# Moving the window block between the two halves of a gathered group, on TensorE and on VectorE

## The reference, cut to what matters

```python
def rgcn_conv(x, src, dst, etype, W, root, bias):
    seg = dst * R + etype
    agg = segment_sum(x[src], seg, n * R)
    cnt = segment_sum(ones, seg, n * R)
    agg = where(cnt > 0, agg / max(cnt, 1), 0).reshape(n, R, -1)
    return einsum('nrd,rdk->nk', agg, W) + x @ root + bias
h = relu(rgcn_conv(h, ..., W1)); h = relu(rgcn_conv(h, ..., W2)); h = relu(rgcn_conv(h, ..., W3))
```

## Time and profile before

| | us |
|---|---|
| median of 3 runs | 5267.58 |
| lowest and highest run | 5249.11, 5267.61 |
| the profiled execution | 5260.04 |
| its span, first to last instruction | 5258.3 |
| mean granted TensorE clock, as a share of full | 0.823 |

### The profile page before, as it was taken

One profiled execution on the slowest core, in us unless ns is written; L12 is line 12 of the kernel. 1 busy time (PEld: TensorE's weight loads), 2 busy tenths in 40 slices (PEclk: granted clock), 3 DMA queues, 4 the chain that ended last, 5 costly groups with the idle time before them and its releaser, 6 DMA issues.

```text
span 5258.3 us, 105311 instructions
## 1 busy us (share of the span) xinstructions
PE 3666.9 (70%) x20468; PEld 2929.5 (56%) x20688; DVE 2687.7 (51%) x6973; ACT 1162.6 (22%) x3868; POOL 2380.1 (45%) x2346
## 2 busy tenths in 40 slices
PE   4777566666777777766767677677777777584872
PEld 1233455555666666555555555566566666574862
DVE  7654344444444444355555555455554554794336
ACT  0122111111111122122222222223322322351112
POOL 0000233344455555466666666566666665002530
PEclk8999777787888888877777778788888888797986
DMA  2022222222333444322323233344444444255740
GB/s 75 33 63 68 73 61 67 74 73 81 97 101 115 121 120 123 108 76 78 86 80 84 81 90 89 105 115 117 126 124 123 129 125 115 104 208 150 203 133 13
DMA packets 478385, 526.90 MB, mean 100 GB/s; under 512 B 96596, under 2 KB 398238, under 8 KB 474670
## 3 DMA queue, kind: packets, MB, share of 16 engines
q1 hardware_dynamic: 252780, 246.52, 15.1%
q0 software_dynamic: 85824, 199.51, 14.0%
q10 hardware_dynamic: 139746, 80.46, 5.2%
HBM read 399.82 MB, written 126.39 MB: 100 GB/s over the span
## 4 chain that ended last, share of the span: by engine, by line
PE 36%; issue 20%; POOL 14%; DMA 13%; DVE 9%; DVEq 3%; ACT 2%; ACTq 1%; SPq 1%; POOLq 0%; another core or an unknown queue 0%
POOL msg_r L608 14%; DMA msg_r<-y_tab,idx_r 9%; PE psum L1566 9%; PE psum L1636 4%; PE psum L1568 2%; DMA msg_r<-x_tab,idx_r 2%; DVE shot_r L1136 2%; PE psum L1747 2%; PE psum L1709 1%; PE psum L1432 1%; PE psum L1494 1%; DVE h_t L1365 1%; PE psum L1748 1%; PE psum L1524 1%; PE psum L1506 1%
## 5 line engine op out<-in xcount | busy, mean ns | idle before, releaser
L608 POOL DMA_INDIRECT msg_r<-y_tab,idx_r x2160 | 2221.9, 1029 | 2223.9 <-issue 1161.6
L1566 PE MATMUL psum<-shot_r 128*128 128x200 f32 x2604 | 1000.1, 486 | 465.1 <-DVE shot_r L1136 437.3
L1130 DVE SCALAR_TENSOR_TENSOR shot_r<-edge_f,win_base,iota 128x600 bf16<-128x600 f32 x434 | 366.4, 844 | 1197.1 <-PE psum L1568 740.7
L684 ACT COPY idx_r<-row_i 128x1 int32 x2142 | 395.6, 190 | 2246.6 <-DMA msg_r<-y_tab,idx_r 2044.3
L1566 PEld LDWEIGHTS psum<-shot_r 128*128 128x128 f32 x2604 | 554.8, 262 | 476.5 <-issue 472.1
L1115 DVE TENSOR_SCALAR hot_r<-iota,edge_g 128x128 f32<-128x128 f32 x1602 | 454.4, 357 | 186.4 <-PE psum L1748 148.8
L1568 PEld LDWEIGHTS psum<-shot_r 128*100 128x100 bf16 x2604 | 444.7, 171 | 115.0
L1568 PE MATMUL psum<-shot_r 128*100 128x128 bf16 x2604 | 462.3, 271 | 0.0
L1747 PE MATMUL psum<-msg_r,shot_r 128*128 128x128 f32 x1440 | 338.1, 321 | 175.3 <-DMA msg_r<-y_tab,idx_r 94.6
L1636 PEld LDWEIGHTS psum<-hot_r,msg_r 128*128 128x128 f32 x2880 | 408.9, 218 | 16.7 <-DMA msg_r<-y_tab,idx_r 6.8
L1636 PE MATMUL psum<-hot_r,msg_r 128*128 128x128 f32 x2880 | 405.8, 300 | 11.3 <-DMA msg_r<-y_tab,idx_r 4.5
(11 more groups left out here) (322 smaller groups left out, 4932.6 us busy)
## 6 DMA issues: line engine op xcount, KB each, us to landing
msg_r<-in_attr SPq DMA_DIRECT2D x882, 64.0 KB
h_t<-count_tab SPq DMA_DIRECT2D x25, 1600.0 KB, 6.6
w_tab<-shot_r ACTq DMA_DIRECT2D x385, 100.0 KB
count_tab<-shot_r ACTq DMA_DIRECT2D x385, 100.0 KB
h_t<-w_tab SPq DMA_DIRECT2D x24, 1600.0 KB, 8.0
msg_r<-y_tab,idx_r POOLq DMA_INDIRECT x2160, 2.6
xn<-heavy_tab SPq DMA_DIRECT2D x76, 320.0 KB
y_tab<-y_s SPq DMA_DIRECT2D x25, 640.0 KB, 2.9
```

Of the source, the lines that this page charges most:

```text
L608: pool.indirect_dma_start(out=msg_r[:, q, 0:width], out_offset=None, in_=table, in_offset=bass.IndirectOffsetOnAxis(ap=idx_r[:, q:q + 1], ...
L684: nc.scalar.copy(idx_r[:, q:q + 1], of[:, q:q + COLS - U + 1][:, bass.ds(c0, 1)]).then_inc(s_idx[k], 1)
L1130: V.scalar_tensor_tensor(out=key_b, in0=of(KEY, KW), scalar=win_base[:, bass.ds(w, 1)], in1=to(KW), op0=ALU.subtract, op1=ALU.is_equal).th ...
L1566: T.matmul(win_ps, low_f[:, i, :], weighted_f[:, i, :], start=False, stop=False)
```

## The change

On TensorE, `window_sums` moves from before the first chunk of a group to before the fourth. On DVE, `window_hots` moves from before the first half of the scaled one-hots to before the second. Both moves are in all three passes. ACT, POOL and SP have the same instructions in the same order as before, and nothing is added or removed. The extra block of each tile in pass 1 and the left-over blocks stay where they are.

```diff
                     dve.wait_ge(s_einv_acc, p)
-                    window_hots(in_pass(dve, 0, p, D, None))
                     for h, half in halves():
+                        if h == 1:
+                            window_hots(in_pass(dve, 0, p, D, None))
                         dve.wait_ge(s_free[0], p * U + half.stop)
                         dve.wait_ge(s_inv_e[h], p)
...
                         group_columns(k, D, p, chunk, plane=slice(INV, INV + 1))
-                        window_hots(in_pass(dve, k, p, D, n_rest))
                         for h, half in halves():
+                            if h == 1:
+                                window_hots(in_pass(dve, k, p, D, n_rest))
                             dve.wait_ge(s_free[k], p * U + half.stop)
                             scaled_hots(k, half, INV).then_inc(s_hot[k][h], 1)
...
                 if k == 0:
                     inverse_counts(p, slot)
-                if k < 3:
-                    window_sums(x)
                 for q in range(U):
+                    if k < 3 and q == UH:
+                        window_sums(x)
                     if q % UH == 0:
```

## The result

The changed kernel takes 5484.0 us (median of 4 runs, 5457.7 to 5493.1) against 5258.3 us (4 runs, 5244.2 to 5267.6): a ratio of 1.0423, with a 95% interval from 1.0377 to 1.047. The profiled execution took 5481.0 us (span 5479.3), 221 more than the 5260.0 of the one before. The forecast was 5320, with a range to 5420: slower was right, the size was not.

A forecast was written before the change was run, and what follows sets the result against it. Pass 0 was taken as bound by a TensorE-DVE ring, passes 1 and 2 by POOL and what it waits for. Terms 160 - 55 - 45 = +60 us on 5260.0 gave 5320 us, range 5225 to 5420.

The forecast's parts named there:

- Pass 0, +160: Pass 0: first groups of tiles +78 us, second groups +86, inner groups -4; +135 to +226 by preparation time.
- the preparation: DVE in pass 0: register work before the block's one-hots, taken as 2.4 us behind three scaled one-hots (2.19 to 2.95).
- The inner ring: Pass 0, 72 inner groups: closed TensorE-DVE chain of 10.29 us, to change by -0.05 us and stay near 10.2.
- Pass 1, -55: Pass 1: POOL's wait before first gathers goes, smaller waits come before fourth gathers; -55 us, bounds -130 and 0.
- 24 x 5.0 going to 24 x 3.8 us: Pass 1 tile ends: wait at the extra block falls from 5.0 to 3.8 us, one block fewer before the third chunk.
- 0.7 us at half clock: Pass 1, fourth gather: loses nothing at full clock, 0.7 us at half; 96 x 0.7 x 0.44 = 30 us.
- Pass 2, -45: Pass 2: the move gains 45 us although the first chunk now waits for ACT's plain one-hots; bounds -110 and +30.
- Of the 163 us over 948 I take 45 away: Pass 2: step that takes 45 us off the 163 us by which the pass exceeds 948 us.
- the ring of two groups: Pass 2: chain from sixth landing through L705, chunks, block and gathers; fits two 7.9 us groups at full clock.
- Rival 2: Wait only moves: fourth gather waits as the first did, pass 0 pays in full; 5395 to 5486, near 5420; chance 0.15.
- Rival 1: Pass 0 inner groups: shorter gap before the block keeps TensorE's clock full, -100 us at most, 5220 us; chance 0.15.
- Rival 3: Waits of passes 1 and 2 nearly vanish (-160) against pass 0's +160, giving 5260 us; chance 0.25.

The follow-up runs named there:

- the first series: First of four measuring series, holding the first four kernels (pass 0, 1 or 2 moved alone; pass 0 with first groups old); kernel before takes 5683.5 us there.
- the late copy: Pass 2 moved, ACT copies the block out after the next group's first plain ones: 5321.0 us, 1.0122; with early attribute transfers too 5235.2 us, 0.9967.
- the early loads: Kernel before with DVE's block register loads ahead of pass 0's wait: 5161.8 us, 0.982; the same with the block moved in pass 0: 5155.6 us, 0.981.

## Why the prediction was right in one pass and wrong in another

**Pass 0, +160: right in sum and cause, partly by luck in the terms.** 166 us were measured, and 115 in the first series. The reason holds: the block's one-hots wait for L1552 and then for the preparation, and with the preparation elsewhere 15 us are left. The inner ring came out as said, 10.24 us; all inner groups together gave 13 us and not 4. Within a tile's start the sizes were off, but not their sum: forecast 17.6 and 13 us, together 30.6; found 15.8 and 15.0, together 30.8. That two errors of 2 us a tile cancel is luck; in the first series the two groups grew by 3.9 and 0.5 us (means). The delay itself was right in both groups, 5.39 and 5.40 us from L1554 to the block against 5.66 and 5.46 forecast, and so was the preparation, 2.35 us for 2.4.

**Pass 1, -55: right in kind, too large.** It gained 22 us by the two traces. Over all profiles but those of the first series the mean is 1112.2 us in four with the block moved and 1130.5 in nine with the old order, 18 us. The tile ends came out as forecast: 24 x 5.0 going to 24 x 3.8 us was the term, 137 going to 101 us was found, although ACT's index copies are now what POOL waits for there. The first gather's wait went too. What was too small is the wait put in its place: 0.7 us at half clock, 30 us in the sum, where 78 us stand before the fourth gathers, in 54 of 120 groups.

**Pass 2, -45: the step that failed.** It was "Of the 163 us over 948 I take 45 away". Measured was +81: 126 us of the 161 by which the profiled execution missed the sum (+221 against +60). The step weighed ACT's 3.3 us to L705 against the ring of two groups, within which the runs show it to be nearly free: 294 us of such waits stood in a pass of 1122.9 us. It did not look at the first and second group of a tile, where the whole loss is, nor at SP at all. There the requests for a tile's second group stand behind the waits for the tile's own loads, and the block had been the work that ran meanwhile. With the first half ahead of the block, the first chunk needs them before they are there. The second group grew by 2.7 us, 24 times 66 us, and when they were asked for early it shrank by 3.8 (12.1 to 8.2); the sum had no such term. The smaller part is ACT's order in a tile's first group, 1.3 us or 31 in all, of which the late copy gave back 21 to 32 us.

**The rivals.** Rival 2 had the size nearly (5395 to 5486, measured 5484) and the wrong place: the loss of pass 2 was not the fourth gather's wait in the middle of a tile but a transfer at its start. In pass 1 its mechanism is there inside the tiles, where 60 us before the first gathers became 78 before the fourth; what the pass gained it gained at the tile ends. Rival 1, the clock, did not come: 0.81 in pass 0 as before. But it came with the early loads. The pause ahead of the block, 2.44 us in the earlier trace rows and 1.96 after the change, fell to 0.46 us, and the clock of the pass was 0.88 and 0.90 with the block moved, 0.85 without. The Trainium skill (TensorE: Matmul & The Clock Gate, section "HAM oscillation — how this bites in real kernels") has idle gaps between bursts as what makes every burst start cold; with that the trace agrees. The higher clock bought nothing that can be told: 1496.9 us at 0.90 against 1493.6 at 0.85, where the block's place differs too. Rival 3, equal gains and price, failed with pass 2.

## What to carry to other kernels

Before a block of work is moved, list everything that was late under its cover on every queue, the DMA requests of the idlest engine among them, and above all at the edges of the outer loop, where an order is different. The longest wait in the list is not the dearest: some 200 us less waiting for ACT gave back 21 us, 95 us less waiting for transfers gave back 75, since the second stood in full before the gathers that set the pace (4.11 us on TensorE, then 4.52 on POOL); one kernel that removes the wait tells them apart. Run the mend in the old order as well: 15 to 28 of these 75 us were no price of the move. And register work ahead of a long operation belongs before the wait, not behind it: three lines moved were worth 100 us in the old order and 252 in the new.

## What the hardware showed that was not expected

The same kernel took 5683.5 us (5674.9 to 5701.8, 13 runs) in the first series, and 5252.8 to 5261.6 in the three others: 8%, more than any edit here is worth. The move in pass 2 cost 49 us in the one and 84 in another. The series ran on chips numbered 4, 3, 4 and 1, so the longest time and one of the short ones stand under the same number, and that the chip makes the difference is not shown. No part of the first series' profiles explains it alone: the gathers' busy time is the same (2221.3 us against 2221.9), pass 0 in the old order takes 1692.6 us at the same clock of 0.81. The shortest landing of a gather is 2.7 us in place of 2.4, the median 2.8 where the other series have 2.6 to 2.8. In pass 1, also in the old order, the granted clock was 0.72 from 2300 to 3300 us, where it was 0.78. Which of these is cause and which effect was not tested.

Taking away what TensorE waits for can leave most of the wait: the clearing product of pass 1 waited 0.9 us in 114 of 120 groups for nothing that the profile shows, where it had waited for a copy before. That TensorE's register work had run under the old wait fits this, and no run tests it.
